# A graph network's preparation phase: memory for counts cleared earlier, memory for sums cleared in the next phase, four input tiles on the way, and one store moved behind others

## The reference

```python
edge_feat = jnp.concatenate([x[src], x[dst], edge_attr], axis=-1)
h = mish(edge_feat @ W1 + b1)
messages = mish(h @ W2 + b2)
agg = jax.ops.segment_sum(messages, dst, num_segments=x.shape[0])
u = mish(jnp.concatenate([x, agg], axis=-1) @ W3 + b3)
out = u @ W4 + b4
y = x + out                      # then a layernorm with gamma and beta
```

## Time and profile before

| | us |
|---|---|
| median of 3 runs | 1329.94 |
| lowest and highest | 1324.53, 1330.15 |
| the profiled execution | 1334.39 |
| its span | 1332.7 |
| TensorE busy in it | 1244.3 (93%) |
| VectorE, ScalarE, GpSimd busy | 1015.5, 851.6, 697.3 |

### The profile page before, as it was taken

How to read it: one execution, slowest core, us unless ns; L and a number is a source line. 1 busy time by engine, 2 the same in 40 slices (tenths; PEclk the granted TensorE clock), 3 DMA queues, 4 the chain that set the end, 5 groups by cost and what they waited for, 6 DMA issues and landing times. The chain is left out here.

```text
span 1332.7 us, 18963 instructions
## 1 busy us (share of the span) xinstructions
PE 1244.3 (93%) x5844; PEld 998.1 (75%) x5844; DVE 1015.5 (76%) x1799; ACT 851.6 (64%) x772; POOL 697.3 (52%) x484
## 2 busy tenths in 40 slices
PE   7974999999999999999999999968799896999998
PEld 6753777777777777787777777756588785888886
DVE  4324799999999999999999999745776247847444
ACT  3204999999999999999999999727633011312210
POOL 0216788888888888888888888117130000011000
PEclk9996999999999999999999999988999997999999
DMA  7997867777877777777777887668200520000001
GB/s 229 329 353 146 169 135 156 154 155 154 159 159 153 149 142 151 155 152 155 155 153 157 159 156 136 193 241 322 85 16 0 190 69 24 17 1 2 0 20 60
DMA packets 108315, 183.59 MB, mean 138 GB/s; under 512 B 35154, under 2 KB 44672, under 8 KB 108248
## 3 DMA queue, kind: packets, MB, share of 16 engines
q0 software_dynamic: 71056, 106.45, 41.4%
q1 hardware_dynamic: 30104, 64.09, 13.9%
q10 hardware_dynamic: 7088, 12.20, 2.8%
HBM read 141.21 MB, written 41.30 MB: 137 GB/s over the span
## 5 line engine op out<-in xcount | busy, mean ns | idle before, releaser
L222 POOL DMA_INDIRECT w_raw<-q_dram,idx_all x172 | 361.1, 2099 | 87.1 <-issue 53.1
L1057 PE MATMUL ps_x<-wA_hi,hT_hi 128*128 128x512 f32 x668 | 270.7, 405 | 1.3 <-DVE hT_lo L747 1.3
L1057 PE MATMUL ps_x<-wA_hi,hT_lo 128*128 128x512 f32 x668 | 264.4, 396 | 0.0
L1057 PE MATMUL ps_x<-wA_lo,hT_hi 128*128 128x512 f32 x668 | 264.1, 395 | 0.0
L222 POOL DMA_INDIRECT w_raw<-p_dram,idx_all x176 | 182.0, 1034 | 109.6 <-issue 108.5
L1057 PEld LDWEIGHTS ps_x<-wA_hi,hT_hi 128*128 128x128 f32 x668 | 125.6, 188 | 34.1 <-issue 2.0
L1057 PEld LDWEIGHTS ps_x<-wA_hi,hT_lo 128*128 128x128 f32 x668 | 125.5, 188 | 30.1
L1057 PEld LDWEIGHTS ps_x<-wA_lo,hT_hi 128*128 128x128 f32 x668 | 125.5, 188 | 28.3
L756 DVE TENSOR_TENSOR x<-ps_x,b 128x512 f32<-128x512 f32 x167 | 114.0, 683 | 26.8 <-PE ps_x L1057 23.0
L1692 POOL TENSOR_TENSOR tmp_n<-X,gam 128x512 f32<-128x512 f32 x10 | 13.9, 1394 | 224.9 <-DVE t_be L1777 180.3
L1016 PE MATMUL ps_x<-ident,w_raw 128*128 128x128 f32 x672 | 103.7, 278 | 20.2 <-issue 12.5
(11 more groups left out here) (270 smaller groups left out, 2858.1 us busy)
## 6 DMA issues: line engine op xcount, KB each, us to landing
ea_raw<-in_eaT SPq DMA_DIRECT2D x88, 128.0 KB
adj_dram<-adj_sb POOLq DMA_DIRECT2D x42, 210.2 KB
adj_dram<-agg_sb ACTq DMA_DIRECT2D x11, 640.5 KB
U_lo<-adj_dram SPq DMA_DIRECT2D x10, 640.0 KB, 8.7
adjT_dram<-adjT_sb SPq DMA_DIRECT2D x10, 640.0 KB, 7.9
adjT_rest<-adjT_dram SPq DMA_DIRECT2D x7, 640.0 KB, 10.0
w_raw<-in_w SPq DMA_DIRECT2D x4, 1024.0 KB, 8.0
w_raw_g<-in_w SPq DMA_DIRECT2D x4, 1024.0 KB, 7.7
```

What stands on the lines that cost most here:

```text
L222: g.indirect_dma_start(G[:, slot, c * D:(c + 1) * D], None, rows, bass.IndirectOffsetOnAxis(ap=idx_all[:, i:i + 1], axis=0), **op).then_in ...
L1057: last = t.matmul(ps_x2[c % 2][:, :], h[:, b.slot, e], w[:, k, :], start=(k == 0 and i == 0), stop=(k == KD - 1 and i == 2))
```

## The change

Three things are changed, all in how memory is moved. No arithmetic changes.

1. The clears of counts' memory start two tiles earlier, at P's second tile. The clears of sums' memory leave the preparation: SP issues them in the edge phase, behind a wait for block 0's first products, ahead of its loads of edge attributes. They have a semaphore of their own, and the first addition to sums' memory and the first write of `agg_sb` wait for it.
2. Three tiles of x are loaded ahead of the index loads, the fourth behind them, and the others each behind a wait for the tile four before it. The store of P's tile 0 no longer stands among them.
3. x turned is stored behind all of Q's stores, in two transfers of 1.5 MB in place of twelve of 256 KB.

```diff
-CLEAR_FROM = 3
+CLEAR_FROM = 1
+X_AHEAD = 4
@@ prepare, SP
                 load_x(0)
                 load_x(1)
+                load_x(2)
                 sp.wait_ge(pad_set, 2)
...
-                for r in range(2, R):
-                    sp.wait_ge(x_in[r - 2], 16)
+                load_x(3)
+                for r in range(X_AHEAD, R):
+                    sp.wait_ge(x_in[r - X_AHEAD], 16)
                     load_x(r)
-                    if r == 6:
-                        store_p(0)
-                for r in range(1, R):
+                for r in range(R):
                     store_p(r)
...
-                    if r >= R - ZE:
-                        i = r - R + ZE
-                        for to, part in zip(xT_dram, (xT_hi, xT_lo)):
-                            sp.dma_start(to[:, cols(i)], part[:, i, :].bitcast(F32)).then_inc(xT_out, 16)
+                for to, part in zip(xT_dram, (xT_hi, xT_lo)):
+                    sp.dma_start(to[:, :], part[:, 0:ZE, :].rearrange("p r d -> p (r d)").bitcast(F32)).then_inc(xT_out, 16)
...
-                sp.wait_ge(xT_out, 32 * ZE)
+                sp.wait_ge(xT_out, 32)
@@ prepare, ScalarE
                 def clear(r):
...
-                    act.dma_start(agg_dram[r * P:(r + 1) * P, :], zeros).then_inc(zero_out, 16)
...
-                    if r == 2:
+                    if r == CLEAR_FROM:
                         act.wait_ge(z_ready, 1)
@@ edge_phase, SP
+                sp.wait_ge(pre_ready, KD)
+                for r in range(DROWS // P):
+                    sp.dma_start(agg_dram[r * P:(r + 1) * P, :], agg_sb[:, 0, :]).then_inc(zero_agg, 16)
                 n = passes(sp, one_pass)
@@ edge_phase, GpSimd
                         if b.k == 0:
-                            wait(zero_out, 32 * (DROWS // P))
+                            wait(zero_out, 16 * (DROWS // P))
...
                 def sum_window(b):
                     if b.real():
+                        if b.k == 0:
+                            wait(zero_agg, 16 * (DROWS // P))
@@ edge_phase, VectorE, window_sums
                         elif b.k == 0:
-                            dve_.wait_ge(zero_out, 32 * (DROWS // P))
+                            dve_.wait_ge(zero_out, 16 * (DROWS // P))
+                            dve_.wait_ge(zero_agg, 16 * (DROWS // P))
```

More of the change, by code:

```diff
@@ L168, in gnn @@
         w3b_in, w4_in, vec_in, zero_out = (sem(n) for n in ("w3b_in", "w4_in", "vec_in", "zero_out"))
+        zero_agg = sem("zero_agg")
         z0_out = sem("z0_out")
@@ L203, in gnn @@
                        h1, Y, w_raw, b3, wA_hi, wA_lo, w3_hi, w3_lo, wc_hi, wc_lo, b2, agg_sb, p_dram, q_dram, agg_dram, adj_dram, eaT, xT_dram,
-                       w03, w04, w3b_in, w4_in, zero_out, p_in, q_in, ea_raw, ea_in, x2, z0_out)
+                       w03, w04, w3b_in, w4_in, zero_out, zero_agg, p_in, q_in, ea_raw, ea_in, x2, z0_out)
         Y += [sb(f"Y{r}", [P, D]) for r in range(2 * KD, R)]
@@ L546, in edge_phase @@
                h1, Z, w_raw, b3, w2_hi, w2_lo, w3_hi, w3_lo, wc_hi, wc_lo, b2, agg_sb, p_dram, q_dram, agg_dram, adj_dram, eaT, xT_dram,
-               w03, w04, w3b_in, w4_in, zero_out, p_in, q_in, ea_raw, ea_in, x2, z0_out):
+               w03, w04, w3b_in, w4_in, zero_out, zero_agg, p_in, q_in, ea_raw, ea_in, x2, z0_out):
     HB = 2 * BE
```

## The result

The changed kernel is slower: 1338.78 us in the median of 6 runs (1336.83 to 1343.42), against 1330.05 (1324.53 to 1331.90) of the kernel before beside it. The ratio is 1.007, 95% interval 1.0051 to 1.0089. That is 0.8 us above the predicted range. The profiled execution was the fastest of the six: 1336.83 us around a span of 1335.2. That of the kernel before had 1334.39 and 1332.7 and was slower than all six of the timed runs beside this kernel, so these two profiles show the difference too small: 2.5 us where the medians have 8.7.

A forecast was written before the change was run, and what follows sets the result against it. DMA engines were taken to bound the preparation from 20 us, TensorE the edge phase. A 13.7 us gain and 12.0 us loss gave -1.7 us, so 1328.2 us from the median; range 1318.5 to 1338.

The forecast's parts named there:

- part 4: Edge phase: sums' clears ahead of block 2's attributes on SP's queue delay h1; loss 12.0 us, bounds 6.1 and 17.5.
- E: First instruction of the edge phase; at 108.7 us before the change, predicted at 95 (bounds 91 and 98), gain 13.7 us.
- part 3: End of preparation: x turned leaves the gaps between Q's stores; Q's eight steps take 21.5 us in place of 31.8.
- part 2: Preparation: filling the DMA hole saves 2 us, full DMA from 15 to 20 us 2, TensorE's x wait 1.9.
- Part 1: Preparation: eleven 256 KB clears of sums' memory taken out, 2.88 MB at 404 GB/s, save 7.1 us of all engines.
- T: TensorE's first product of block 1 in the edge phase, at 123.53 us in the kernel before's first profile; no forecast term.
- Behind E: Edge phase: TensorE sets the line, so any shift of its start arrives at the kernel's end one to one.
- The sum: Whole kernel: gain 13.7 us and loss 12.0 us give -1.7 us, a span of 1331.0 for 1332.7.
- B: Edge phase: clears slow in strict turns with adding gathers, landing E + 28 or later, loss 17.5, 1337 us; chance 0.14.
- Rival C: Preparation: SP waits for x turned or Q's slots stay late; E at 102, gain 6.7, 1335 us; chance 0.15.
- A: Edge phase: clears pass quickly, block 2's attributes land at E + 16.6, loss 6.1, 1320.0 us; chance 0.19.
- D: Edge phase: the load of block 2's attributes is not on the path, VectorE has room; 1316 us; chance 0.05.

The follow-up runs named there:

- Part 4 alone: The kernel before with only the clears of sums' memory moved from the preparation to SP's queue in the edge phase; 1340.34 us, ratio 1.0081 to the kernel before.
- attributes first: The changed kernel with block 2's and 3's edge attributes loaded ahead of the clears of sums' memory on SP's queue; 1325.45 us, 0.9969 of the kernel before.

## Why the prediction was wrong, point by point

The path was right, and two terms of the sum were mis-sized, both toward a faster kernel. The loss of part 4 was put at 12.0 us and measured 14.9 to 16.3, because block 2's adding gathers had been left out of what passes ahead of its attributes. The gain in E was put at 13.7 us and measured 11.6 in one profile and about 8 in three others with the same preparation, because part 3 let the gathers' data begin 2.2 us behind their issue and E follow 5 us behind the last engine, while with x turned ahead of them they began only 6.4 us behind it, and because part 2 counted work saved that wasn't.

- **Part 1**, 7.1 us: right as far as the scatter of E tells. Part 4 alone moved E by 7.2 and 6.3 against the two profiles of before.
- **Part 2**, 2 us for the hole, 2 for a full DMA from 15 us, 1.9 of TensorE's: wrong. The share from 15 to 20 us stayed at 0.58, and the hole took 0.3 MB more than before (103 GB/s for 25 over 4 us), not 0.8. With clears two tiles earlier ScalarE waited 6 to 8 us for weights whose loads share the engines with them, and taking them back beside attributes first gave 3.0 us, which the intervals hardly tell from nothing. The four tiles of x gave 0.9 us, inside the intervals. I had priced bytes moved forward as work saved and hadn't asked whose load they would stand beside. What this part did to the weights is not wholly clear: part 4 alone, with clears from the fourth tile, waited 7.8 us too, and with both the fourth tile and four tiles of x ahead it is 3.1 to 3.7.
- **Part 3**, the order on SP's queue: half right. VectorE's wait for Q's slots fell from 13.7 us to 3.1 in the first profile, but only to 6.3, 8.6 and 10.5 in the other three with this preparation; the tenth evacuation ended at 77.2 there and near 80.2 in those, for 74.0 (77 with slots late), and GpSimd gathered from 80.16 and from 83.0 to 83.4 for 78.5. SP's wait for x turned, which was to end near 90 and to come last, was over near 86.5 by the sizes of the packets. What came last was the gathers' data, which I had from 80.7 on and which began only when x turned had passed, at 86.6, and went on until 94.9. E follows their end, not an engine's or SP's wait: by 2.2 us here, in the kernel before (data to 106.5, E at 108.7) and, within 0.2 us, in every other profile, while it came 9.8 us behind the end of GpSimd's fourth gather (87.32), where I took 5. With x between Q's stores the way from the first gather to E was 3.4 us shorter. Together: the gain in E was 11.6 us in the first profile and 8.45 in the second, against 13.7 (bounds 10.7 and 17.7).
- **Part 4**, the mechanism: right in each step. The queue's order, VectorE's order, the split's releaser, TensorE's wait for h1 are all in the rows, and the split's landing + 2.8 is h1 (3.0 taken).
- **Part 4**, the size: wrong. I let 13.8 us of engine work pass ahead of the landing at E + 22.5 and left block 2's adding gathers out, on the reasoning that strict turns were only a bound. They took turns: 3.14 MB passed from 105.9 to 122.7, 187 GB/s. In these 16.8 us q0 held the engines for 8.8 (I had 6) and q1 for 9.0 (I had 7.8), and the split started at E + 25.7, 26.8, 25.6 and 27.1 in the four profiles, between the E + 22.5 taken and the E + 28 of strict turns. The loss, as the shift of T - E against the 14.9 of before, was 14.9 to 16.3 us, not 12.0.
- **Behind E**, one to one: right, span - T is the same within 5 us over shifts of T of 20.
- **The sum**, -1.7 forecast: +3.4 at h1 in the first profile (-11.6 + 15.0) and +7.6 in the second (-8.45 + 16.04), +8.7 in the medians. The nearest rival was B, whose time was 1337, but that its time is so near is partly luck: its loss of 17.5 wasn't reached, and the gain was below its own 10.7. Two terms of opposite sign and twelve us each left a difference whose sign hung on the errors of both. The deciding rate of 165 GB/s that I gave for B went with a gain of 10.7. At 8.5 the same working (6.6 us over nothing, a loss of 15.1, a landing at E + 25.6, 3.14 MB in 16.8 us) gives 187 GB/s, which is what the queue had; the profiled loss was at that edge.
- **Rival C** had a share as well: E was above 100, the sign that I had named for being wrong, in three of the four profiles with this preparation, Q's slots stayed late in them, and x turned held the end of the preparation, though by holding back the gathers' data and not by SP's wait. Rivals A and D fell.

## What to carry to other kernels

Before moving bulk stores to an "idle" moment, look for the small load that the same queue issues next and for the engine that waits for it; put such loads ahead of the bulk, which here cost nothing that can be seen (T - E 15.0 against 14.9) and turned +0.7% into -0.3%. Price bytes that share the engines with adding gathers at the gathers' own pace (0.12 MB per us each here), taken from a stretch with both queues full. Look for the first byte of a gather in the queues' rows and not only for its issue: large stores on another queue held it back by 4 us here. Where a forecast is the small difference of two large terms, let the chances of both signs follow from the two terms' bounds.

## What the runs showed of the hardware

Two queues that both had much work sent about as many packets each (442 and 407, 357 and 352), though a packet of an adding gather holds an engine longer. In the kernel after the engines moved 384 GB/s from 114 to 118 us with the clears and plain gathers, and 254 from 118 to 123 with adding gathers beside SP's queue; q0 took 71.8% of the engines for 0.65 MB and q1 36.2% for 0.61 MB. The stores beside them cost the adding gathers little: block 0's four took 8.3 us with 1 MB of the node part's stores beside them and 8.5 in the kernel before, nearly alone.

Two stores of 1.5 MB on SP's queue held back the first data of gathers issued behind them on another queue: 6.4 to 6.5 us from the first issue to the first data in the eight profiles with x behind Q, 2.2 to 2.3 in the five with x between Q's stores. Putting x between Q's stores in pieces of 256 KB, with nothing else changed, is enough for the difference (6.4 and 2.3); whether the size or the place of the stores makes it, no run tells. E came 2.2 us behind the last data of these gathers in twelve profiles and 2.4 in the one where it is VectorE's first instruction.

The profiles don't show that the long stall cost TensorE more clock than the short one. Windows of after around the restart; the number ahead of the DMA share is the granted clock (0.50 is 1.2 GHz, 1.00 is 2.4):

```profile
129.00:131.00 2.00, 2.00 (x10) 1.70 (x9) 1.28 (x2) 1.31 (x2) 0.00 (x0) 0.50 0.00 0
131.00:133.00 2.00, 2.00 (x13) 1.69 (x12) 0.29 (x1) 0.29 (x1) 0.00 (x0) 0.99 0.00 0
```

The same windows of the kernel before:

```profile
127.00:129.00 2.00, 2.00 (x10) 1.70 (x9) 0.00 (x0) 0.00 (x0) 1.70 (x2) 0.55 0.66 106
129.00:133.00 4.00, 4.00 (x21) 2.94 (x19) 2.37 (x7) 3.12 (x2) 3.09 (x4) 1.00 0.87 125
```

Both restart at half clock, and it is back 4 us after T in the one (22.5 us of standing) and 5 us in the other (7.6 us). In the second profile of each it is 6 us (23.9 us of standing) and 3 us (8.3), so the spread within a kernel is as large as any difference between them.
